# Whole-array turns moved beside the other whole-array products, the spectral mix one step later, and the second variance of 14 tiles on ScalarE

## The reference, cut to what matters

```python
# x: (32, 1024), cut into 64 patches of 16 -> 2048 tokens of width 256
h = silu(x_cat @ W_h.T + b_h) @ W_o.T + b_o + x_cat @ W_r.T + b_r      # patch embedding
n = layernorm(h)                                                       # over the 256 features
q, k, v = n @ Wq.T, n @ Wk.T, n @ Wv.T         # per head: 16 heads of width 16
h = h + softmax(q @ k.T / 16) @ v @ W_out.T + b_out                    # 64 tokens attend to each other
n = layernorm(h)
h = h + real(ifft(fft(n) @ (w_real + i w_imag))) + bias                # spectral mix
```

## Time and profile before

| | |
|---|---|
| median of three runs | 141.29 us |
| the profiled execution | 141.65 us |
| its span, first to last instruction | 139.8 us |
| TensorE clock granted | 1.00 in every slice |
| busy share: PE, PEld, DVE, ACT, POOL | 95%, 80%, 80%, 61%, 68% |
| chain that ended last | PE 83%, DVE 6%, DMA 3%, issue 2% |

### The profile page before, as it was taken

The page is one execution under the profiler, slowest core; times in us unless marked ns, Lnnn a source line. Parts: engine busy times, 40 slices in busy tenths (PEclk is TensorE's granted clock), DMA queues, the critical chain, the costliest instruction groups (busy, mean ns, idle before and its releaser), DMA issues.

```text
span 139.8 us, 6135 instructions
## 1 busy us (share of the span) xinstructions
PE 132.5 (95%) x2444; PEld 111.9 (80%) x2444; DVE 112.0 (80%) x337; ACT 85.8 (61%) x245; POOL 94.9 (68%) x186
## 2 busy tenths in 40 slices
PE   6679999999999998999999999999999999999991
PEld 2269999999998877878889888788888887887650
DVE  5574697949978597798898988988989889879671
ACT  4374766567888395847748659477476494663410
POOL 3285795997574455587696876876867868764751
PEclk9999999999999999999999999999999999999999
DMA  3678000021000011112203213123032031122012
GB/s 70 157 171 249 31 0 0 0 28 19 2 0 5 5 9 14 19 42 23 56 8 61 46 15 61 40 23 65 2 59 51 10 61 42 19 55 50 3 38 75
DMA packets 24508, 5.89 MB, mean 42 GB/s; under 512 B 20384, under 2 KB 24224, under 8 KB 24480
## 3 DMA queue, kind: packets, MB, share of 16 engines
q1 hardware_dynamic: 24192, 5.37, 18.3%
q10 hardware_dynamic: 288, 0.13, 0.3%
HBM read 2.35 MB, written 2.10 MB: 32 GB/s over the span
## 4 chain that ended last, share of the span: by engine, by line
PE 83%; DVE 6%; DMA 3%; issue 2%; POOL 1%; ACT 1%; SPq 1%; DVEq 0%
PE bank L1054 11%; PE bank L972 11%; PE bank L1040 7%; PE bank L1096 6%; PE bank L1116 6%; PE bank L977 5%; PE bank L1103 4%; PE bank L1149 4%; PE bank L1084 4%; DMA wf_raw<-in_W_r 3%; PE bank L1067 2%; PE bank L1162 2%; PE bank L966 2%; PE bank L1120 2%; PE bank L1153 2%
## 5 line engine op out<-in xcount | busy, mean ns | idle before, releaser
L829 DVE TENSOR_REDUCE bank<-bank 128x4 f32<-128x256 f32 x64 | 22.8, 425 | 6.9 <-ACT pT L378 6.4
L378 ACT ACTIVATE pT<-bank 128x256 f32<-128x256 f32 x64 | 19.4, 389 | 2.5 <-PE bank L1067 2.5
L1054 PE MATMUL bank<-qT,xzT 32*128 32x64 f32 x512 | 17.9, 276 | 0.0
L1054 PEld LDWEIGHTS bank<-qT,xzT 32*128 32x128 f32 x512 | 15.7, 186 | 2.7 <-issue 2.7
L700 DVE TENSOR_TENSOR hid_lo<-bank,hid_hi 128x512 fp32r<-128x512 f32 x16 | 11.0, 686 | 7.2 <-ACT bank L346 7.2
L587 POOL TENSOR_TENSOR side_lo<-sideT,side_hi 128x256 fp32r<-128x256 f32 x14 | 10.2, 729 | 8.1 <-ACT sideT L389 8.1
L548 POOL TENSOR_SCALAR xblk<-xh,parity_sb 128x128 f32<-128x128 f32 x32 | 11.6, 375 | 5.8 <-PE bank L1103 4.7
L373 ACT ACTIVATE maxT<-bank 128x128 fp32r<-128x128 f32 x16 | 4.4, 277 | 17.8 <-PE bank L1076 17.8
L598 POOL TENSOR_TENSOR on_lo<-onT,on_hi 128x256 fp32r<-128x256 f32 x14 | 10.3, 737 | 7.1 <-ACT on_hi L393 6.9
L556 POOL TENSOR_TENSOR hb_all<-h_all,bout_bc 128x256 f32<-128x256 f32 x16 | 11.6, 738 | 4.0 <-ACT h_all L350 4.0
L341 ACT ACTIVATE hid_hi<-bank 128x512 fp32r<-128x512 f32 x16 | 9.6, 598 | 4.2 <-PE bank L966 4.1
(11 more groups left out here) (170 smaller groups left out, 386.1 us busy)
## 6 DMA issues: line engine op xcount, KB each, us to landing
out<-y SPq DMA_DIRECT2D x16, 128.0 KB, 1.7
xblk<-xh SPq DMA_DIRECT2D x32, 32.0 KB, 2.5
wo_raw<-in_W_o SPq DMA_DIRECT2D x1, 512.0 KB, 4.3
wout_raw<-in_W_out SPq DMA_DIRECT2D x1, 256.0 KB, 3.0
fr<-in_wr SPq DMA_DIRECT2D x1, 256.0 KB, 4.4
fi<-in_wi SPq DMA_DIRECT2D x1, 256.0 KB, 4.6
minus_raw<-in_minus_rows SPq DMA_DIRECT2D x1, 128.0 KB, 2.1
bout_bc<-in_b_out SPq DMA_DIRECT2D x1, 128.0 KB, 3.5
```

The lines of the kernel that those rows point to most:

```text
L378: nc.scalar.activation(pT[:, j, :], bank[j][:, D:2 * D], ACT.Exp).then_inc(exp_done, 1)
L829: nc.vector.tensor_reduce(rowmax[:, j, :], bank[j][:, 0:D].rearrange("p (h k) -> p h k", k=TOK), AX_X, ALU.max).then_inc(max_done, 1)
L1054: pe.matmul(bank[j][:, at0:at0 + TOK], xzT[t % 3][rows32, 2 * half + b, :, :].rearrange("p e k -> p (e k)"), qT[t % 3][rows32, half, TOK * ...
```

## The change

- PE: the three turns no longer stand ahead of `scores`. `turn_side(i-1)` stands between `query` and `project`, `turn_x` and `turn_max` behind `project`, ahead of `weigh(i+1)`. They are those of one tile later (`turn_x(i+4)`, `turn_max(i+2)`). The first step is written out.
- `mix_freq` and `finish` are of tile `i-2` instead of `i-1`; SP stores `i-3`.
- `h2` is turned into the bank of the weighing (`side_of`), so `turn_side` also waits for `on_set`, and `weigh` for `side_copied`.
- For the first 14 tiles the variance of `h2` is made by ACT in two passes with an accumulated sum, `sum_row` and `sum_squares`, with POOL's `mean2` between them; DVE's statistics remain for the last two.
- `WHOLE_ON` is 15: tile 14 is projected by the split form too. `xh` has three buffers.

The diff, cut to its core:

```diff
-WHOLE_ON = 14
+WHOLE_ON = 15
+ROWS_ON_ACT = 14
@@ ACT
+            def sum_row(t):
+                act.wait_ge(h2_done, t + 1)
...
+                nc.scalar.activation(unread[:], h2[t % 2][:], ACT.Copy, accum_out=sum2[:]).then_inc(sum2_done, 1)
+            def sum_squares(t):
+                act.wait_ge(mean2_done, t + 1)
...
+                nc.scalar.activation(unread[:], h2[t % 2][:], ACT.Square, bias=neg_mean2[:],
+                                     accum_out=squares2[:]).then_inc(squares2_done, 1)
             def step(i):
-                if i + 1 < T:
-                    copy_max(i + 1)
-                if i >= 1:
-                    copy_side(i - 1)
                 if i + 3 < T:
-                    copy_xT(i + 3)
                     copy_xzT(i + 3)
+                if 1 <= i <= ROWS_ON_ACT:
+                    sum_row(i - 1)
+                    sum_squares(i - 1)
                 if i < WHOLE_ON:
                     lead_on(i)
                 if i + 1 < T:
                     exponent(i + 1)
                 if i + 3 < T:
                     copy_q(i + 3)
+                if i >= 1:
+                    copy_side(i - 1)
+                if i + 4 < T:
+                    copy_xT(i + 4)
+                if i + 2 < T:
+                    copy_max(i + 2)
@@ POOL
+            def mean2(t):
+                pool.wait_ge(sum2_done, t + 1)
...
+                nc.gpsimd.tensor_scalar(neg_mean2[:], sum2[:], -1.0 / D, None, ALU.mult).then_inc(mean2_done, 1)
@@ POOL step(i), behind place_same(i + 2)
+                if 1 <= i <= ROWS_ON_ACT:
+                    mean2(i - 1)
+                if 1 <= i < T:
+                    add_bias(i - 1)
+                if i < WHOLE_ON:
+                    split_on(i)
+                if i + 5 < T:
+                    normalize(i + 5)
                 if 1 <= i <= WHOLE_SIDE:
                     split_side(i - 1)
...
+                if i >= 1:
                     inv_std2(i - 1)
@@ DVE step(i)
                 divide(i)
-                if i >= 1:
-                    variance2(i - 1)
...
-                if 1 <= i < T - 2:
-                    finish(i - 1)
+                if 2 <= i < T - 2:
+                    finish(i - 2)
@@ PE
             def turn_side(t):
                 pe.wait_ge(h2_done, t + 1)
+                if t < T - 2:
+                    pe.wait_ge(on_set, t + 2)
@@ PE weigh(t)
+                if t >= 2:
+                    pe.wait_ge(side_copied, t - 1)
@@ PE project(t)
+                if t == T - 2:
+                    pe.wait_ge(y_set, t - 1)
```

More of the change, by code:

```diff
@@ L131, in audio_tower_kernel @@
         idle_rows = sb("idle_rows", [P, HID], BF16)
-        xh = [sb(f"xh{i}", [P, D]) for i in range(2)]
+        xh = [sb(f"xh{i}", [P, D]) for i in range(3)]
         xblk = [sb(f"xblk{i}", [P, 2, D]) for i in range(2)]
@@ L246, in at, with side_of @@
             return isinstance(i, int) and i == n
+        def side_of(t):
+            return bank[PV_BANK][:, 0:D] if t < T - 2 else bank[MAX_BANK][:, D:2 * D]
         def has(t):
@@ L304, in _ @@
             place_crossed(1)
-            for i in range(T + 1):
+            for i in range(T + 3):
                 if i + 2 < T:
                     place_crossed(i + 2)
-                if i >= 1:
-                    store(i - 1)
+                if i >= 3:
+                    store(i - 3)
             for par in range(2):
@@ L382, in copy_side @@
                 if t == T - 1:
-                    nc.scalar.activation(last_sideT[:], bank[SIDE_BANK][:, D:2 * D], ACT.Copy).then_inc(side_copied, 1)
+                    nc.scalar.activation(last_sideT[:], side_of(t), ACT.Copy).then_inc(side_copied, 1)
                     return
                 if t < WHOLE_SIDE:
-                    nc.scalar.activation(side_hi[:], bank[SIDE_BANK][:, D:2 * D], ACT.Copy).then_inc(side_hi_set, 1)
+                    nc.scalar.activation(side_hi[:], side_of(t), ACT.Copy).then_inc(side_hi_set, 1)
                 if t >= 1:
                     act.wait_ge(side_lo_set, t)
-                nc.scalar.activation(sideT[:], bank[SIDE_BANK][:, D:2 * D], ACT.Copy).then_inc(side_copied, 1)
+                nc.scalar.activation(sideT[:], side_of(t), ACT.Copy).then_inc(side_copied, 1)
             def lead_on(t):
@@ L444, in _ @@
             lead_mix_weights()
+            copy_xT(3)
+            copy_max(1)
             for i in range(T + 1):
@@ L899, in step @@
                     split_max(i + 2)
+                if i == T - 2:
+                    finish(i - 2)
                 residual(i)
-                if 1 <= i < T - 2:
-                    finish(i - 1)
+                if 2 <= i < T - 2:
+                    finish(i - 2)
             dve.wait_ge(zeros_set, 3)
@@ L1083, in turn_side @@
                 for half in range(HALF):
-                    last = pe.transpose(bank[SIDE_BANK][:, D + half * P:D + (half + 1) * P],
+                    last = pe.transpose(side_of(t)[:, half * P:(half + 1) * P],
                                         h2[t % 2][:, half * P:(half + 1) * P], ident[:])
@@ L1195, in step @@
             def step(i):
-                if 0 <= i + 2 < T:
+                if i + 2 < T:
                     scores_inputs(i + 2)
-                if i >= 1:
-                    turn_side(i - 1)
-                if 0 <= i + 1 < T:
-                    turn_max(i + 1)
-                if 3 <= i + 3 < T:
-                    turn_x(i + 3)
-                if 0 <= i + 2 < T:
-                    scores(i + 2)
-                if 0 <= i + 1 < T:
-                    keyed_scores(i + 1)
-                    take_max(i + 1)
-                if 1 <= i < T - 2:
-                    mix_freq(i - 1)
-                if i >= 0:
-                    project(i)
-                if 0 <= i + 3 < T:
-                    query(i + 3)
-                if i == -1:
-                    cols_spectrum(1)
-                if 0 <= i + 1 < T:
-                    weigh(i + 1)
+                    scores(i + 2)
+                keyed_scores(i + 1)
+                take_max(i + 1)
+                if i >= 2:
+                    mix_freq(i - 2)
+                if i + 3 < T:
+                    query(i + 3)
+                turn_side(i - 1)
+                project(i)
+                if i + 4 < T:
+                    turn_x(i + 4)
+                if i + 2 < T:
+                    turn_max(i + 2)
+                weigh(i + 1)
             for t in range(2, T):
@@ L1257, in _ @@
             cols_spectrum(0)
-            for i in range(-1, T - 1):
+            turn_max(0)
+            scores_inputs(1)
+            scores(1)
+            keyed_scores(0)
+            take_max(0)
+            query(2)
+            cols_spectrum(1)
+            weigh(0)
+            turn_x(3)
+            turn_max(1)
+            scores_inputs(2)
+            scores(2)
+            keyed_scores(1)
+            take_max(1)
+            query(3)
+            project(0)
+            turn_x(4)
+            turn_max(2)
+            weigh(1)
+            for i in range(1, T - 1):
                 step(i)
```

67 lines of the change are left out of this document (42 added, 25 removed).

## The result

Six executions of the changed kernel have a median of 150.81 us (149.46 to 151.86), the kernel before 141.25 beside them. The ratio is 1.065 (95% interval 1.0619 to 1.0681); it is of the fast executions, without the slow one of 151.86. The sign of the forecast was right; its 147.1 was 3.7 us short, and the range ended at 149.6.

The account below looks back on a forecast made before the run. TensorE's order of work was taken to bound the middle steps, then a closed ring of 5.85 us in the new order. Adding +1.2, +3.9 and +0.7 us gave 147.1 us, 8-in-10 range 143.8 to 149.6.

Parts of the forecast that it names:

- The sign of the forecast: Whole kernel: the change makes it slower, given a chance of 0.89.
- The ring: Middle steps: weighing, division, exponentials, maxima, turn, next weighing form a closed chain of 5.85 us; +3.9 us over thirteen steps.
- first step: Tile 0 to 1: the same wait for the maxima makes it 6.14 us instead of 4.92, +1.2 us.
- last: Tile 14 to 15: the weighing newly waits for `side_copied`, 5.0 us instead of 4.32, +0.7 us.
- What TensorE itself saves: Weighing to scores without turns: 0.1 us less per step, so PE alone could run a step in 5.45 us.
- the first rival: Middle steps: the chain is shorter than added up, PE stays the bound and the gain is real, 140.0 us; chance 0.08.
- The wait at the turn of the maxima: Ahead of `turn_max`: PE reaches it at 5.24 us, can start at 5.64, and waits 0.40 us each step.
- The variance: Second variance on ACT: two passes of 0.42 and 0.53 us stay hidden, with 0.30 us to spare.
- my two prices: Accumulated output on ACT: costs between nothing and 0.20 us as its own instruction, covered by both.
- the cover of 0.30: ACT ahead of `on_hi`: squares let it go at 2.56 us, due at 2.86; the one thin cover.
- The third rival: ACT's passes: accumulator reads of 0.5 us behind each exceed their cover and delay `on_hi`, 149.9 us; chance 0.06.
- The sum: Whole kernel: +1.2, +3.9 and +0.7 give +5.8 us on 141.65, a median of 147.1 us.

Follow-up runs that it names:

- experiment 1: Changed kernel with the eight long warm-up products replaced by 78 short ones, moving all later PE instructions 70 products back: 147.07 us, ratio 1.040.
- experiment 5: Changed kernel with the turn of the maxima behind the weighing again and 78 short warm-up products for the eight long: 143.64 us, ratio 1.0132.
- 11: Changed kernel with the maxima's turn behind the weighing, 78 short warm-up products, and the second variance on DVE: 143.58 us, ratio 1.0143.
- experiment 4: Changed kernel with the variance of all tiles back on DVE, ACT without its two passes: 150.7 us, ratio 1.0659.
- 3: Changed kernel with the turn of the maxima directly behind the weighing instead of ahead, its copy behind that of `xzT`: 146.93 us, ratio 1.0381.
- 9: Changed kernel with the eight long warm-up products replaced by 105 of 48 columns, 97 more products ahead of the loop: 152.08 us, ratio 1.0743.
- 7: Kernel before with only the turn of the maxima moved ahead of the weighing, its copy to the step's end: 151.86 us, ratio 1.0727.
- 10: Kernel before with the turn of the maxima ahead of the weighing and 74 short warm-up products for the eight long: 152.06 us, ratio 1.0742.
- experiment 12: Changed kernel with three idle products of 512 columns between weighing and scores in each step: 155.84 us, ratio 1.1017.
- 2: Changed kernel without SP's crossing transfers from tile 2 on (output not the reference's): 150.0 us, ratio 1.0617.
- experiment 6: Kernel before with its eight long warm-up products replaced by 74 short ones: 141.32 us, ratio 0.9974.

## Why the prediction was wrong

**The ring: right.** Step 5.81 against 5.85, first step 6.12 against 6.14, last 5.07 against 5.0, whose weighing is released by `sideT` as said. The links are within 0.05 us of what the earlier trace rows gave, but for the turn behind the split, 0.06 instead of 0.15, which is the bound of the earlier trace rows. Experiments 1 and 5 differ by the ring alone: 2.7% of 141.3, 3.8 us. In that is what the closed ring passes on, the 0.5 us of the two late steps of experiment 1.

**What TensorE itself saves: wrong in sign.** I had 5.45 us for PE alone, 0.1 less than before; it is 5.63 (experiments 5 and 11). (The 5.55 of before was a mean over unlike steps, 6.01 with a wait of 0.39, eleven of 5.56 and 5.00; that does no harm.) The direct change from the weighing to the scores costs 0.15 (forecast 0.21); that a change of tiling mode costs a drain of TensorE, as the Trainium skill has it (TensorEngine Tiling (Array Packing), Key Properties), agrees with both numbers, and the first rival, which rested on it, still fell. The turns are what I mis-sized. In the kernel before the small products and the whole-array ones (mix, projection, queries) part the step thus:

```profile
82.54:84.25 1.71, 1.71 (x46) 1.00 0.00 0
84.25:86.15 1.90, 1.90 (x73) 1.00 0.44 95
86.15:88.11 1.96, 1.96 (x20) 1.00 0.16 17
```

and in experiment 5 thus (weighing and one turn; scores, keyed scores and maxima; all the rest):

```profile
82.23:83.50 1.27, 1.27 (x42) 1.00 0.05 13
83.50:85.40 1.90, 1.90 (x73) 1.00 0.19 17
85.40:87.85 2.45, 2.45 (x23) 1.00 0.28 67
```

Four turns took 0.44 us out of the first stretch and brought 0.49 into the last. Behind the pair of `h` one product takes 0.21 us to the next (86.71 to 86.92) instead of 0.12. Moved to stand beside whole-array products the turns share their shape but not their type: they are f32 between fp32r products. That the type is the reason is a guess; no run changes it alone. The wait at the turn of the maxima in an undisturbed step is so 5.81 - 5.63 = 0.18, not 0.40. For the forecast's time this error is harmless, since the ring sets the step. With the ring open it is a part of what is left instead of a gain: of the 1.9 us of experiment 5 its trace has 0.5 in the thirteen middle steps and 1.3 in the first and the last (5.45 and 5.10 against 4.92 and 4.32). The first rival was wrong twice over.

**The variance: right in size, without reserve.** The squares start 2.26 us behind the weighing (forecast 2.15), and the accumulator is read by an instruction of its own, 0.19 to 0.22 us, the upper of my two prices. `on_hi` then starts at 130.64 with `onT` done at 130.60: the cover of 0.30 is used up just so. In undisturbed steps nothing is lost (experiments 4 and 11), but nothing is left over either: where POOL was late, in two steps of experiment 1, the passes cost 0.19 and 0.31 us. I had named this the one thin cover and gave it no term for a late POOL. The rule of the Trainium skill that I quoted for VectorE (VectorE: DVE Perf Modes, Two Vector instructions with no wait between them) holds for ScalarE in this trace, and in undisturbed steps its price stays hidden. The third rival gave 149.9, near the result, by reads of 0.5 us in every step; they take 0.19 to 0.22.

**The sum: the step that failed.** "Thirteen steps: 13 x 5.85" takes it for granted that PE starts when its operands are there. There is no term for the fetch of its instructions, and in the earlier trace rows none is visible, for before PE never stopped by "issue" in the loop. It is nearly the whole difference: experiment 1 takes all but one of the pauses away and measures 147.07 for a forecast of 147.1. That the two agree to the last digit is in part luck. Against the trace of before, experiment 1 starts its first weighing 0.5 us earlier, which I had not forecast, and its undisturbed steps are 0.04 below 5.85, 0.5 in thirteen; the two late steps give 0.5 back.

In the profiled execution the pauses are 2.8 us in five steps. The median lies 1.35 above that execution, and this part is open. A low clock is not enough for it: three of the other five executions have mean clocks of 0.977 to 0.989, and in experiments 3 and 9 the low clock followed pauses of 0.82 and 0.93 us, but two have a mean clock of 1.00 and still took 150.47 and 150.79. Longer pauses at the same products could do it, as in the execution of experiment 4 (151.02 us, 4.2 us in five steps); no trace of the changed kernel shows them.

By ratios: the order of PE and the ends of the loop 1.3% (experiment 5), the ring 2.7% (1 less 5), the pauses with what hangs on them 2.5% (the changed kernel less 1); 1.9 + 3.8 + 3.5 = 9.2 us.

**Why the order of before is spared** is shown in part. A pause comes where a border falls into the keyed scores or the maxima, or just behind them, and the next block is then too late. Two things differ. In the changed kernel the 112 small products of a step run with nothing between; at 0.02 to 0.03 us each PE passes through half a block in about 1.5 us, less than the 2.2 to 3.0 from packet to first product behind a pause. Before, 0.7 us of turns stand in the middle, in experiments 7 and 10 0.6. Experiment 12 shows that time there halves the loss in the three steps compared. And the packet comes later in the work: ahead of the pauses it starts 39 to 80 products behind the border last passed, mostly 53 or more; in the kernel before it is at most 40, if its borders stand at the same counts, which without pauses no row shows. That alone isn't enough either: experiment 5 has 54 and 56 without a pause, one with its border just behind the maxima, the other with the whole-array products ahead of it, as far as the counts hold. I found nothing that sets this lateness: it isn't the crossing transfers (2), and PE's waiting at the turn doesn't do it alone (10). It stays open.

No kernel run here beats the one before by more than the 0.26% of experiment 6.

## What to carry to other kernels

Before an instruction is moved ahead of another, follow what it waits for round the loop: if that depends on the other one's previous turn, the ring's length is the new step, and its links can be added from rows of the old trace (here to 1%). Ask of each cover how late its slowest supplier can be, not only how late it is in a quiet step. Price moved products beside their new neighbours before counting a saving. And when TensorE runs at its own limit with long stretches of small products, count products up to each "issue" pause: equal distances mean blocks of instructions. Some more products ahead of the loop show what they cost, but take two different numbers: 70 removed all pauses but one here, 97 brought five others.

## What the runs showed of the hardware

- PE's instructions come in blocks of 125 products with their weight loads, one 16 KB packet each; from the start of the packet to the block's first product it was 2.2 to 3.0 us where PE stood waiting for it.
- 70 more idle products ahead of the loop made the changed kernel 2.3% faster (1.040 against 1.065), 97 more did not (1.0743).
- Behind pauses of 0.82 and 0.93 us the granted clock stood at 0.50 for some 3 us; behind ones of 0.97 and 1.21 (experiments 2 and 4) it stayed at 1.00.
- A read of ACT's accumulator is an instruction of its own: 0.21 us (median) behind the sum, 0.19 behind the squares.
